# Selective scan on one Trainium2 core: GpSimd forms half of the state products, from a copy of the output factors

## The reference, cut to what matters

```python
dbc = jnp.einsum('ble,ep->blp', x, x_proj_w)
dt_r, Bm, Cm = jnp.split(dbc, [R, R + N], axis=-1)
dt = jax.nn.softplus(jnp.einsum('blr,re->ble', dt_r, dt_proj_w) + dt_proj_b)
A = -jnp.exp(A_log)

def step(h, inp):
    x_t, dt_t, B_t, C_t = inp
    dA = jnp.exp(dt_t[..., None] * A)
    h = dA * h + dt_t[..., None] * B_t[:, None, :] * x_t[..., None]
    y = jnp.einsum('ben,bn->be', h, C_t)
    return (h, y)
```

## Time and profile before

| | |
|---|---|
| median of 3 runs | 2509.95 us (2505.46 to 2511.80) |
| profiled execution, its own time | 2501.56 us |
| span of the instructions in it | 2499.8 us |
| busy in the span: PE, DVE, ACT, POOL | 78%, 66%, 41%, 23% |
| mean granted TensorE clock | 0.825 |
| scan loops of the four rows | from 1838 to 2242 us |

### The profile page before, as it was taken

The page is one execution under the profiler, slowest core; times in us unless marked ns, Lnnn a source line. Parts: engine busy times, 40 slices in busy tenths (PEclk is TensorE's granted clock), DMA queues, the critical chain, the costliest instruction groups (busy, mean ns, idle before and its releaser), DMA issues. The chain is left out here.

```text
span 2499.8 us, 31121 instructions
## 1 busy us (share of the span) xinstructions
PE 1946.5 (78%) x11378; PEld 1099.6 (44%) x11378; DVE 1644.7 (66%) x3698; ACT 1030.2 (41%) x1610; POOL 584.6 (23%) x520
## 2 busy tenths in 40 slices
PE   4787887878787877799899767778876766689973
PEld 2453634445363232367676545555532222233321
DVE  6666657575666454453536797895469998985566
ACT  1236464564644343343333223233245345334561
POOL 0003323241321010010001353531025534631000
PEclk8888999999898677899999778866567776798975
DMA  4002122130302000000000000000000000000000
GB/s 158 1 1 64 35 52 47 26 72 18 81 1 88 1 1 1 1 22 1 1 1 1 1 1 1 1 1 1 0 0 1 0 0 0 0 1 1 1 5 13
DMA packets 19223, 43.77 MB, mean 18 GB/s; under 512 B 5323, under 2 KB 7935, under 8 KB 18175
## 3 DMA queue, kind: packets, MB, share of 16 engines
q1 hardware_dynamic: 19071, 41.78, 5.9%
HBM read 16.59 MB, written 1.05 MB: 7 GB/s over the span
## 5 line engine op out<-in xcount | busy, mean ns | idle before, releaser
L2185 PE MATMUL lane_banks<-l_attn_lane_hc,base 128*128 128x512 f32 x256 | 176.8, 809 | 98.4 <-DVE l_attn_lane_hc L2336 98.4
L2261 POOL TENSOR_TENSOR l_attn_lane_u<-l_attn_lane_xp,l_attn_lane_bn 128x512 f32<-128x512 f32 x128 | 177.1, 1409 | 207.7 <-ACT l_attn_lane_bn L2237 203.5
L2327 DVE TENSOR_TENSOR_SCAN l_attn_lane_h<-l_attn_lane_da,l_attn_lane_u 128x512 f32<-128x512 f32 x128 | 187.4, 1493 | 7.7 <-POOL l_attn_lane_u L2261 3.9
L1577 ACT ACTIVATE l_ffn_lane_hT<-lane_banks,weights 128x512 f32<-128x512 f32 x128 | 88.0, 687 | 153.3 <-PE lane_banks L1533 153.0
L543 POOL TENSOR_SCALAR lane_next_rstd<-lane_next_mv 128x4 f32<-128x4 f32 x48 | 12.1, 253 | 587.3 <-DVE lane_next_mv L529 587.2
L1385 ACT ACTIVATE l_attn_lane_ex<-lane_banks 128x1024 f32<-128x1024 f32 (+3 forms) x128 | 87.2, 702 | 139.9 <-PE lane_banks L1343 139.6
L2185 PEld LDWEIGHTS lane_banks<-l_attn_lane_hc,base 128*128 128x128 f32 x256 | 57.6, 246 | 178.9 <-DVE l_attn_lane_hc L2336 139.6
L1555 PEld LDWEIGHTS lane_banks<-weights,l_ffn_lane_hT 128*128 128x128 f32 x1024 | 121.4, 193 | 24.3 <-issue 21.1
L1623 DVE SCALAR_TENSOR_TENSOR l_ffn_lane_eo<-lane_banks,l_ffn_lane_sel,l_ffn_lane_eo 128x128 f32<-128x128 f32 x224 | 63.0, 344 | 103.9 <-PE lane_banks L1555 103.5
L1555 PE MATMUL lane_banks<-weights,l_ffn_lane_hT 128*128 128x128 f32 x1024 | 124.2, 278 | 5.6 <-DVE l_ffn_lane_eo L1623 4.4
L2237 ACT ACTIVATE l_attn_lane_bn<-lane_banks 128x512 f32<-128x512 f32 x64 | 38.0, 595 | 203.5 <-PE lane_banks L2179 200.8
(11 more groups left out here) (528 smaller groups left out, 4699.4 us busy)
## 6 DMA issues: line engine op xcount, KB each, us to landing
f_attn_lane_work<-f_attn_lane_work SPq DMA_DIRECT2D x256, 64.0 KB, 2.0
weights<-packed SPq DMA_DIRECT2D x1, 4564.5 KB, 19.5
f_attn_lane_vb<-f_attn_lane_va SPq DMA_DIRECT2D x8, 512.0 KB, 4.5
f_attn_lane_vb<-f_attn_lane_va SPq DMA_DIRECT2D x8, 384.0 KB, 5.9
weights<-packed SPq DMA_DIRECT2D x1, 2320.0 KB, 8.5
weights<-packed SPq DMA_DIRECT2D x1, 2091.0 KB, 12.9
out<-x SPq DMA_DIRECT2D x4, 256.0 KB, 2.2
weights<-packed SPq DMA_DIRECT2D x1, 897.0 KB, 9.1
```

Of the source, the lines that this page charges most:

```text
L1577: act.activation(hT[:, n % 2, c, :], ps(c), ACT.Relu, bias=w("m1_b1", b, b + 1)).then_inc(*s.up("hidden_ready"))
L2185: pe.matmul(ps(2 + c), w("ident"), hc[:, c, :], start=(n == 1), stop=(n == NS)).then_inc(*s.up("state_added"))
L2261: g.tensor_tensor(u[:, i % 3, :], dtx[:, c, :], bn[:, n % 2, :], ALU.mult).then_inc(*s.up("u_ready"))
L2327: v.tensor_tensor_scan(h[:, c, :], da[:, i % 3, :], u[:, i % 3, :], 0.0, ALU.mult, ALU.add).then_inc(*s.up("scanned"))
```

## The change

For the second chunk (c = 1) the product with C moves from DVE to GpSimd. GpSimd's operand is not the PSUM bank but a new SBUF tile `cn`, into which ACT copies bank 1 for each state; DVE's product for the first chunk reads `cn` too. GpSimd's product of state n-1 is issued behind its two `u` of state n. `hc_ready` now counts DVE's products and `weighed` GpSimd's. `cn` has one buffer: ACT's copy for the next state waits for both products of this one. The broadcast of C waits for the last copy (`cn_ready`) where it waited for nothing of its own.

```diff
+    cn = sb("cn", [P, T])
...
             if n >= 1:
                 for c in range(C):
                     yield
-                    pe.wait_ge(*s.at("hc_ready", C * (n - 1) + c + 1))
+                    pe.wait_ge(*s.at("hc_ready" if c == 0 else "weighed", n))
                     pe.matmul(ps(2 + c), w("ident"), hc[:, c, :], start=(n == 1), stop=(n == NS)).then_inc(*s.up("state_added"))
             if n < NS:
+                yield
+                if n >= 1:
+                    pe.wait_ge(*s.at("cn_ready", n))
                 pe.matmul(ps(1), net.w16("part16")[0:96, NS + n:NS + n + 1].to_broadcast([96, P]), parts[:, :], start=True, stop=True)\
                   .then_inc(*s.up("c_in_psum"))
...
                 act.activation(da[:, i % 3, :], dt[:, c, :], ACT.Exp, scale=net.a3[:, c, n:n + 1]).then_inc(*s.up("da_ready"))
+            yield
+            act.wait_ge(*s.at("c_in_psum", n + 1))
+            if n >= 1:
+                act.wait_ge(*s.at("weighed", n))
+                act.wait_ge(*s.at("hc_ready", n))
+            act.activation(cn[:, :], ps(1), ACT.Copy).then_inc(*s.up("cn_ready"))
...
+
+        def weigh(n):
+
+            yield
+            g.wait_ge(*s.at("scanned", C * n + 2))
+            g.wait_ge(*s.at("cn_ready", n + 1))
+            if n >= 1:
+                g.wait_ge(*s.at("state_added", C * n))
+            g.tensor_tensor(hc[:, 1, :], h[:, 1, :], cn[:, :], ALU.mult).then_inc(*s.up("weighed"))
+
         for n in range(NS):
             for c in range(C):
...
                 g.tensor_tensor(u[:, i % 3, :], dtx[:, c, :], bn[:, n % 2, :], ALU.mult).then_inc(*s.up("u_ready"))
+            if n >= 1:
+                yield from weigh(n - 1)
+        yield from weigh(NS - 1)
...
                 if n >= 1:
-                    v.wait_ge(*s.at("hc_ready", C * (n - 1) + c + 1))
+                    v.wait_ge(*s.at("hc_ready" if c == 0 else "weighed", n))
                 v.tensor_tensor_scan(h[:, c, :], da[:, i % 3, :], u[:, i % 3, :], 0.0, ALU.mult, ALU.add).then_inc(*s.up("scanned"))
             yield
-            v.wait_ge(*s.at("c_in_psum", n + 1))
-            for c in range(C):
-                i = C * n + c
-                yield
-                v.wait_ge(*s.at("scanned", i + 1))
-                if n >= 1:
-                    v.wait_ge(*s.at("state_added", C * (n - 1) + c + 1))
-                v.tensor_tensor(hc[:, c, :], h[:, c, :], ps(1), ALU.mult).then_inc(*s.up("hc_ready"))
+            v.wait_ge(*s.at("cn_ready", n + 1))
+            v.wait_ge(*s.at("scanned", C * n + 1))
+            if n >= 1:
+                v.wait_ge(*s.at("state_added", C * (n - 1) + 1))
+            v.tensor_tensor(hc[:, 0, :], h[:, 0, :], cn[:, :], ALU.mult).then_inc(*s.up("hc_ready"))
```

## The result

| | before | after |
|---|---|---|
| median of the runs | 2507.70 us (4 runs, 2503.78 to 2511.80) | 2576.98 us (4 runs, 2574.91 to 2578.00) |
| profiled execution, its own time | 2501.56 us | 2577.34 us |
| span | 2499.8 us | 2575.5 us |

The ratio of the changed kernel to the one before is 1.0277, 95% interval 1.0259 to 1.0294: 69 us more, where 54 were summed and 2560 us forecast. Between the two profiled executions it is 76 us. The time lies within the stated range.

The account below looks back on a forecast made before the run. The prediction took DVE's queue as the bound of the 402 us of scan loops. It summed 38 + 15 + 1 = +54 us, giving 2555.6 or 2564, and forecast 2560 us, 2% slower, range 2512 to 2606.

Parts of the forecast that it names:

- DVE is the bound; POOL's time beside two-operand work costs DVE 0.85 us each: Scan loops: DVE busy 362 of 402 us; each POOL operation meeting a scan costs DVE 1.99 - 1.14 = 0.85 us.
- A round goes from 8.65 to 11.2 us: Both lanes scanning: one state of each lane; all six POOL operations meet two-operand work, 10.9 us plus a little for handovers.
- 15 rounds: Both lanes scanning, two stretches of 29 scans each: 15 x (11.2 - 8.65) = +38 us.
- The three stretches beside a preamble, +15: One lane scanning, the other in its preamble: +2.7 us of DVE time and 2 for waits, +5 us a stretch.
- The last stretch, +1: Lane 1 scans row 3, lane 0 is in the next block, mostly reading PSUM: 0 to +1 us.
- ACT's copies are hidden: Scan loops: 64 copies at 0.60 us, 38 us added to ACT, hide behind DVE.
- Nothing absorbs it after 2242 us: After the scan loops: both lanes end late by about the same, so what follows does not change.
- The faster one: Both lanes scanning: only two of POOL's six operations a round meet scans, round 7.5 us; 2483 us in all, chance 0.08.
- The chain rival: Scan loops: the one-buffer chain `weighed`, copy, `bn`, `u`, product bounds; +1.3 us for 34 states, 2605 us, chance 0.11.

Follow-up runs that it names:

- narrow_u_before: The kernel before with GpSimd's `u` written for 64 of 512 columns (all but the first three of each row): 2456.53 us, ratio 0.9808.
- copy_alone: The kernel before plus ScalarE's copy of C, which nothing reads; VectorE's products wait for it but read PSUM: 2492.71 us, ratio 0.9951.
- the narrow one: The changed kernel with GpSimd's product written for 64 of 512 columns, except in each row's first state: 2523.00 us, ratio 1.0081.
- The memset: The changed kernel with GpSimd's product replaced by a memset of the same tile, except in each row's first state: 2528.34 us, ratio 1.0097.

## Why the prediction was right, and where its sizes were off

- *DVE is the bound; POOL's time beside two-operand work costs DVE 0.85 us each.* Right. The step of a scan in the double stretches is 2.0 us (4.08 for two) against 1.99 read before, and narrow_u_before shows that the collisions were there before the change.
- *A round goes from 8.65 to 11.2 us.* It is 11.35. The split into its parts holds too: 10.37 with the operand alone, 10.3 to 10.7 with POOL's product alone, 9.2 to 9.3 with POOL's product taken away.
- *15 rounds.* Mis-sized. The prediction noted that the new order has eight rounds in each stretch and then summed 15. With 16 rounds a double stretch takes 91 us; the two measured 184 against 131, +53 where +38 was summed. A part of it is states that were scanned beside a preamble before: 58 scans lay in the double stretches, now 64. It is also why the stretches of the earlier trace rows and of the result do not hold quite the same work.
- *The three stretches beside a preamble, +15.* Measured +22, with 51 scans in them in place of 53. The terms were of the right kind (SBUF products that meet POOL, POOL products that meet scans); DVE's idle time in these three grew by 8 us (28 to 36), where 2 us a stretch were set for waits.
- *The last stretch, +1.* It stayed at 64 us, with four scans fewer and 9 us more of idle time on DVE.
- *ACT's copies are hidden.* Right as to the copy itself: copy_alone is no slower than before. In the changed kernel DVE waits 14.9 us for the copy, 17 times, because the copy waits for PE.
- *Nothing absorbs it after 2242 us.* Right: from the end of the scans to the end of the span it was 258 us before and is 255.
- *The rivals.* The faster one needed at most three of POOL's six operations in a round to meet anything; in the double stretch from 1930 to 2010 us none of POOL's is as short as when alone (`u` at least 1399 ns, the product 2174, against 1.09 us). The chain rival is wrong as the bound: DVE's busy time grew and its idle time in the double stretches is 9 us of 184. As a part it is not refuted. The prediction's chain led from `weighed` straight to the copy and left out the way over PE, and it set 6 us for waits beside the preambles and 0.3 us a round for the handover, 10 in all; DVE's idle time grew by 22. The sum was 54 us against 69 on the medians and 76 between the profiled executions; the mechanism was right, while the count of rounds and the waits were set too low.
- *The rule weighed in the prediction* (the Trainium skill, SBUF — State Buffer, "Who interferes with whom") asked for strict turns, 2.23 us for a scan that meets an `u`. The moved product comes near to that: it takes 2174 ns in the median, twice the 1.09 us of a `u` alone, and the narrow one is held up for 0.9 us to do 0.3. The scans step at 2.0 us, so the rule is a little too hard in size: by an estimate from these steps (1.14 + 1.09 - 2.0) about 0.2 us of a POOL operation does not stand in DVE's way. The memset shows the other half of the rule, that a GpSimd operation which only writes isn't held up.

## What to carry to other kernels

Before work goes from VectorE to GpSimd, look in VectorE's timeline for one instruction that comes in two durations, and see whether GpSimd's work lies beside the longer ones. If it does, the two engines share what you hoped to double, and moving an operation adds it to the same queue. Then ask of each new wait what stands in front of it in an in-order queue: here a second buffer changed nothing, because the copy hung on PE. The cheap remedy, tried here once, is the opposite one: keep or put one operand of VectorE's long operations in PSUM (here a scan from PSUM never slowed, and the round fell from 8.65 to 7.4 us); copying an operand from PSUM to SBUF so that GpSimd can read it takes this protection from VectorE's own operations too (44 to 57 us here).

## What was not expected of the hardware

The size of the operand's effect: four products took 2.5 us from PSUM and 5.1 from SBUF, with the same work on GpSimd. That GpSimd's memset of 128 x 512 beside full scans keeps 514 to 525 ns. And that ScalarE's unused copy with VectorE's products waiting for it made the kernel 0.5% faster (2492.7 us), which stays unexplained.
